# Ten instead of eight head pairs' score maxima in the expert phase of an attention-and-experts kernel, and the output bank zeroed there

## What is computed

```python
zn = layernorm(xn) * ln_w + ln_b
q, k, v = split(zn @ W_qkv + b_qkv)            # 16 heads of 8 columns
attn = softmax(q @ k.T / sqrt(8), over keys)   # 4 batches, 1024 x 1024 per head
s = xn + concat(attn @ v) @ W_proj + b_proj
h = gelu(xn @ W1[e] + b1[e])                   # 8 experts, 512 hidden units
ffn = sum_e weights[:, e] * (h @ W2[e] + b2[e])  # weights: softmax over the top 2 of 8
out = x + s * silu(ffn)
```

## Time and profile before

| | |
|---|---|
| median of three runs | 1101.2 us (1100.84 to 1102.49) |
| the profiled execution's own time | 1103.0 us |
| its span, first to last instruction | 1101.2 us |
| mean granted TensorE clock | 0.988 |
| first exponential (attention begins) | 513.36 us |
| start of block 240 (no more singles) | 1049.36 us |
| PE, DVE, ACT busy over the span | 93%, 80%, 79% |
| PE busy time of matmuls, us | 1029.3 |

### The profile page before, as it was taken

How to read it: one execution, slowest core, us unless ns; L and a number is a source line. 1 busy time by engine, 2 the same in 40 slices (tenths; PEclk the granted TensorE clock), 3 DMA queues, 4 the chain that set the end, 5 groups by cost and what they waited for, 6 DMA issues and landing times.

```text
span 1101.2 us, 17451 instructions
## 1 busy us (share of the span) xinstructions
PE 1029.3 (93%) x5865; PEld 444.1 (40%) x5897; DVE 883.7 (80%) x1589; ACT 866.9 (79%) x1190; POOL 368.0 (33%) x555
## 2 busy tenths in 40 slices
PE   4998999999999999999999999999999999999997
PEld 3675666666666666664222222122222121122222
DVE  5647877787878787765999899989998998899943
ACT  6876667676767677666898998989898989798985
POOL 4786656657666667554001000001000001000010
PEclk9999999999999999999999999999999999999998
DMA  6432221414142232324212221212112221122102
GB/s 183 123 99 68 66 83 31 120 30 121 31 107 50 64 80 51 97 51 120 51 44 53 55 53 39 68 40 54 42 52 51 56 53 42 51 53 54 25 24 82
DMA packets 99410, 72.02 MB, mean 65 GB/s; under 512 B 21693, under 2 KB 83834, under 8 KB 99322
## 3 DMA queue, kind: packets, MB, share of 16 engines
q1 hardware_dynamic: 99322, 70.92, 24.5%
HBM read 53.12 MB, written 15.46 MB: 62 GB/s over the span
## 4 chain that ended last, share of the span: by engine, by line
PE 34%; ACT 8%; DVE 7%; issue 2%; SPq 1%; DMA 0%; POOL 0%; ACTq 0%; DVEq 0%; POOLq 0%
PE psum L1055 17%; PE psum L1034 8%; ACT p_ring L869 8%; PE psum L999 7%; DVE neg_max_half L1318 7%; PE psum L1084 1%; ACT o_sb L860 1%; DMA den<-o_sb 0%; SPq L469 0%; PE psum L1098 0%; PE psum L1010 0%; SPq L473 0%; DVE neg_max_rest L1327 0%; DVE y L1379 0%; POOL h_lo L685 0%
## 5 line engine op out<-in xcount | busy, mean ns | idle before, releaser
L869 ACT ACTIVATE p_ring<-psum 128x1024 f32<-128x1024 f32 x512 | 494.8, 1026 | 59.7 <-PE psum L1034 54.3
L1318 DVE TENSOR_REDUCE neg_max_half<-psum 128x1 f32<-128x512 f32 x768 | 481.6, 681 | 44.5 <-PE psum L999 36.7
L1055 PE MATMUL psum<-p_ring,v_sb 128*9 128x512 f32 x2048 | 269.2, 598 | 0.4 <-ACT o_sb L860 0.3
L823 ACT ACTIVATE h_hi<-psum,cols 128x512 fp32r<-128x512 f32 x192 | 132.4, 690 | 132.2 <-PE psum L949 131.2
L999 PE MATMUL psum<-k_max_stack,q_max_stack 48*128 48x512 bf16 x768 | 202.2, 380 | 16.6 <-DVE neg_max_half L1318 16.3
L1336 DVE TENSOR_REDUCE neg_max_half<-psum 128x1 f32<-128x512 f32 x256 | 169.3, 683 | 51.7 <-PE psum L985 45.0
L685 POOL TENSOR_TENSOR h_lo<-h_split,h_hi 128x512 fp32r<-128x512 f32 x128 | 165.1, 1294 | 135.4 <-ACT h_split L826 135.2
L1034 PE MATMUL psum<-q_stack,k_stack 51*128 51x512 bf16 x1024 | 200.0, 386 | 3.4 <-ACT p_ring L869 2.2
L635 POOL CAST neg_max_parts<-neg_max_rest 128x16 bf16<-128x16 f32 x32 | 6.3, 197 | 493.6 <-DVE neg_max_rest L1327 493.5
L1034 PEld LDWEIGHTS psum<-q_stack,k_stack 51*128 51x128 bf16 x1024 | 49.5, 93 | 299.2 <-ACT p_ring L869 276.2
L947 PE MATMUL psum<-xn_t_hi,w_hi 128*128 128x512 f32 x256 | 144.8, 566 | 0.7 <-DVE neg_max_half L1336 0.5
(11 more groups left out here) (129 smaller groups left out, 957.5 us busy)
## 6 DMA issues: line engine op xcount, KB each, us to landing
expert_w_bc<-expert_w_dram SPq DMA_DIRECT2D x64, 256.0 KB, 5.1
k_rows_dram<-qk_parts SPq DMA_DIRECT2D x24, 256.0 KB, 3.1
q_max_stack<-q_rows_dram SPq DMA_DIRECT2D x64, 96.0 KB, 2.5
k_max_stack<-k_rows_dram SPq DMA_DIRECT2D x64, 96.0 KB, 2.5
q_stack<-q_rows_dram SPq DMA_DIRECT2D x64, 96.0 KB, 2.4
k_stack<-k_rows_dram SPq DMA_DIRECT2D x64, 96.0 KB, 2.5
q_rows_dram<-qk_parts SPq DMA_DIRECT2D x8, 384.0 KB, 2.6
xz<-in_L_attn_z_dram SPq DMA_DIRECT2D x8, 256.0 KB, 3.2
```

Of the source, the lines that this page charges most:

```text
L823: act.activation(hh[:, (g * HS + j) % HR, :], up, ACT.Gelu, bias=col(C_B1 + i))\
L869: act.activation(p_sb[:, n % PR, a, :, :].rearrange("p h t -> p (h t)"), scores_bank[s % 2], ACT.Exp, scale=SCALE).then_inc(S("P"), 1)
L1055: i = pe.matmul(o_bank[at:at + VR, :], v_sb[:, b * KT + kt, 2 * (p % PB) + hh, :], p_sb[:, n % PR, a, hh, :], start=(kt == 0), stop=(kt == ...
L1318: dve.tensor_reduce(mx[:, p % MXR, c, hh * NT + t:hh * NT + t + 1], ring_bank(("max", u)), AX.X, ALU.max, negate=True).then_inc(S("R"), 1)
```

## The change

The first ten pairs' maxima are taken in the expert phase, in the same slots 36 to 251: 320 instead of 256, so 104 of these 216 slots have two (40 before) and the others one. The transpositions' slots are set anew. In the attention phase 704 singles are left instead of 768; they are issued from block 2 to 239 instead of 0 to 239, so that a block has 3 (228 blocks) or 2 (ten blocks) where before it had 3 (192 blocks) or 4 (48). 22 transpositions are left in it instead of 24. The blocks in which a pair is complete move: SP's loads and stores of the maxima move with them. The zeroing of the output bank goes from the head of DVE's attention list to slot 226, behind a wait for the last use of that bank.

```diff
--- before.py
+++ after.py
@@ -182,9 +182,10 @@
 
 
         MAXES = [(p, t, c) for p in range(PAIRS) for t in range(NT) for c in range(2)]
-        EARLY_PAIRS = 8
+        EARLY_PAIRS = 10
         EARLY = EARLY_PAIRS * 4 * NT
         BLOCKS = PAIRS * KT
+        MAX_FROM = 2
         MAX_BLOCKS = BLOCKS - 2 * KT
         RING = []
         ring_at = {}
@@ -194,7 +195,8 @@
 
         def singles_upto(n, half):
 
-            upto = [min(len(SINGLES), -(-((n + a) * len(SINGLES)) // MAX_BLOCKS)) for a in range(2)]
+            upto = [min(len(SINGLES), -(-max(0, n + a - MAX_FROM) * len(SINGLES) // (MAX_BLOCKS - MAX_FROM)))
+                    for a in range(2)]
             return (upto[0], min(upto[0] + 2, upto[1]), upto[1])[half]
 
         def done_block(p):
@@ -223,9 +225,10 @@
                 on_ring(item)
         ENDS_FROM = BLOCKS - 2 * KT + 3
 
-        EARLY_AT = [HT + 4 + (27 * m) // 32 for m in range(EARLY)]
+        EARLY_AT = [HT + 4 + (27 * m) // 40 for m in range(EARLY)]
         EARLY_DONE = [EARLY_AT[(p + 1) * 4 * NT - 1] for p in range(EARLY_PAIRS)]
-        EARLY_TURN = [2 * HT + 2, 2 * HT + 28, 3 * HT + 26, 4 * HT + 26, 5 * HT + 26, 6 * HT + 26, 7 * HT + 5, 8 * HT + 1]
+        EARLY_TURN = [g * HT + at for g, at in ((1, 28), (2, 26), (3, 26), (3, 30), (4, 26), (5, 26), (5, 30), (6, 26),
+                                                (7, 9), (7, 30))]
         EARLY_MIN = [d + 2 for d in EARLY_DONE]
 
         def ring_bank(item):
@@ -547,19 +550,20 @@
                     sp.wait_ge(S("qp_st"), 2 * QP_ST)
                     for p in range(2):
                         sp_max_rows(sp, p)
-                if g in (2, 3):
-                    sp_max_rows(sp, g)
+                for p in {2: [2], 4: [5], 6: [8]}.get(g, []):
+                    sp_max_rows(sp, p)
                 if g + 1 < NG:
                     sp_load_x(sp, g + 1)
                 spread_w(g)
-                if g > 2:
-                    sp_max_rows(sp, g + 1)
-                for p in ([], [], [0], [1], [2], [3], [4], [5, 6])[g]:
+                for p in {2: [3], 3: [4], 4: [6], 5: [7], 6: [9]}.get(g, []):
+                    sp_max_rows(sp, p)
+                for p in {2: [0], 3: [1], 4: [2, 3], 5: [4], 6: [5, 6], 7: [7, 8]}.get(g, []):
                     sp_store_max(sp, p)
+            sp_max_rows(sp, EARLY_PAIRS)
             for p in range(2):
                 sp_score_rows(sp, p)
                 sp_load_max(sp, p)
-            sp_store_max(sp, 7)
+            sp_store_max(sp, EARLY_PAIRS - 1)
             sp.wait_ge(S("qp_st"), NG * QP_ST)
             sp_max_rows(sp, EARLY_PAIRS + 1)
             sp.wait_ge(S("m2"), NG * HT)
@@ -1340,7 +1344,12 @@
             def lo(ns):
                 return [lambda n=n: weights_lo(dve, n) for n in ns]
 
-            beside = {}
+            def o_zero():
+
+                dve.wait_ge(S("vd"), NG)
+                dve.memset(o_bank[:, :], 0.0).then_inc(S("o_zero"), 1)
+
+            beside = {(NG - 1) * HT + 2: [o_zero]}
             for m in range(EARLY):
                 beside.setdefault(EARLY_AT[m], []).append(early_max(m))
             for p in range(EARLY_PAIRS):
@@ -1402,7 +1411,6 @@
                 ends.setdefault(4 * g + 2, []).append(lambda g=g: finish(g))
 
             dve.wait_ge(S("vd"), NG)
-            dve.memset(o_bank[:, :], 0.0).then_inc(S("o_zero"), 1)
             for n in range(BLOCKS):
                 halves, turns = block_items(n)
                 p, kt = divmod(n, KT)
```

## The result

The changed kernel takes 1106.12 us (median of five runs, 1104.33 to 1107.32); its ratio to the kernel before is 1.0037 [1.0026, 1.0048]. The forecast was 1096 and a small gain; it is a small loss. The profiled execution took 1104.33 us, span 1102.5, clock 0.993. TensorE, VectorE and ScalarE are busy for 93, 79 and 79% of it.

What follows compares the result with a forecast made beforehand. TensorE was taken to pace the expert phase, ScalarE the attention blocks with three singles. 14.1 + 11 + 1 - 2.4 - 34.7 + 6.2 = -4.8 us from 1103.0 gave 1098.2, by median 1096, range 1083 to 1108.

Steps and rivals of the forecast that it cites:

- I take +11: Expert phase: VectorE's crowding by 64 added reductions (full slots, waits for two banks) costs +11 us.
- 64 x 0.22 = +14.1: Expert phase: TensorE's own work for 64 further maxima at 0.22 us each, +14.1 us.
- I take +1: Turns (transpositions of pairs' maxima): a 3.2 us stop before slot 254, partly regained elsewhere; +1 us, between -2 and +3.
- E as a whole, +26: E, the stretch from slot 32's `up` to the first exponential, grows by 26 us.
- -2.4: Start of attention: without memset and singles in blocks 0 and 1, the first blocks take 6.3 us; -2.4 us.
- -34.7: Attention, blocks 3 to 239: with three singles or two per block, 492.6 instead of 527.3 us; -34.7 us.
- +6.2: Attention, SP at kt = 2: late denominators in five pairs make VectorE, then TensorE wait; +6.2 us, 0 to 12.
- TensorE's wait near 23: Expert phase: TensorE's total wait for the early maxima's reductions, 12.2 us before, comes near 23.
- the second (1105): Rival, VectorE binds the expert phase: TensorE's waits for reductions grow by 19.5 us; 1105 us, chance 0.25.
- The third: Rival, attention: denominators come late in more pairs, 12 us lost instead of 6.2; 1102 us, chance 0.10.
- the fourth: Rival: TensorE binds both phases, attention gives back only 7 us; 1124 us, chance 0.04.
- the gaps take the reductions: Rival, expert phase: VectorE's idle gaps absorb added reductions, +3 instead of +11, late denominators cost 2; 1084 us, chance 0.20.

Runs made afterwards that it cites:

- e3: Changed kernel (ten early pairs) with each early reduction over 256 of its 512 keys, the other half left out: 1094.32 us, ratio 0.9935.
- e4: Kernel before (eight early pairs) with each early reduction over 256 of its 512 keys: 1094.12 us, ratio 0.9926.
- e6: Changed kernel with the same 320 early maxima, second ones mainly in slots 3 and 0 modulo four, three turns later: 1076.69 us, ratio 0.977.
- e10: Changed kernel with VectorE's low half of the split one slot later in its list, no maximum moved: 1088.11 us, ratio 0.9883.
- e8: Kernel before (eight early pairs) with memset in slot 226, singles from block 2, SP's sums and denominators first: 1099.63 us, ratio 0.998.
- e5: Changed kernel again, unaltered, on a second chip: 1103.35 us, ratio 1.0019 to the kernel before.
- e1: Changed kernel with pair 9's turn back in the tail (slot 257 instead of 254): 1100.04 us, ratio 0.9984.
- e7: Changed kernel with second maxima in better slots, pair 9's turn in the tail, and SP's sums and denominators first: 1067.54 us, ratio 0.9692.
- e2: Changed kernel with SP's issues of sums and denominators ahead of its loads and stores of maxima: 1099.01 us, ratio 0.9965.
- e12: Kernel before with memset in slot 226, singles from block 2, SP's sums first, and 40 second maxima in slots 3 modulo four: 1090.76 us, ratio 0.9904.

## Why the prediction was wrong, point by point

- **"I take +11" for VectorE, the step that failed: its size held by luck, its reason did not.** It said that a further maximum pays its whole reduction where VectorE is full, and that the 12.2 us of waits grow with the double slots. Measured, 28.4 us of E less 14.1 and less 3.0 for the turns leave 11.3. But with VectorE 61 us less busy the 64 maxima still cost 26.4 instead of 28.4 us (e3, e4), and with as many doubles the waits are 2.4 us instead of 17.6 and E 25.9 us shorter (e6). Without a maximum moved, the low half one slot later in VectorE's list gives 14.2 us (e10). The price is one of the order in VectorE's list, and a term for that was missing. "64 x 0.22 = +14.1" for TensorE's own work was not tried by itself: well placed, 64 maxima cost 10.6 us in all.
- **What a further maximum costs, from the trace.** e8 has the early maxima in the places of the kernel before. In its groups 1 to 6 the time from the start of the matmul ahead to a maximum's start is 77.1 us over 224 maxima (0.344 each), in e5 101.5 over 280. The 56 further ones cost 24.4 us, 0.44 each, and the groups themselves are 24.6 us longer (400.0 against 375.4).
- **"I take +1" for the turns: mis-sized.** A wait of 3.2 us in slot 254 was forecast, and 3.09 came; 2.5 to 3.8 are a loss (e1). Not foreseen was pair 0's turn, four slots behind its last maximum, where TensorE waited 1.41 us; pair 2's 0.52 came in the first profile and not in e5. Less 1.63 and 0.36 that went at pairs 1 and 6, the waits grew by 3.0, the upper bound given.
- **E as a whole, +26: measured +28.4 and +30.0.** The turns are 2 us of the 2.4 above the forecast. Of the 28.4, 22.5 lie in groups 1 to 6 and 5.9 behind slot 224.
- **"-2.4" for the start of attention: -1.7** (6.99 instead of 8.72 us). e8, with eight pairs, the early memset and the empty blocks, has 7.22. No run tries the memset or the empty blocks alone. The forecast of 6.3 us took no account of the clock: before and after, 3.4 us of this stretch are at 1.2 GHz; e7, with none, takes 5.77.
- **"-34.7" and "+6.2": right.** Blocks 3 to 239 took 499.5 us, forecast 492.6 + 6.2 = 498.8. The late denominators came in pairs 4, 11, 15 and 27 (1.42, 1.06, 0.95, 1.35 us of VectorE's wait) and not in pair 8; in four other pairs before block 240 VectorE waited about 0.5. e2 puts them at 5.4 to 7.3 us in all.
- **"TensorE's wait near 23", "first exponential about 539".** 18.7 and 544.05; 2.2 of the latter lie before slot 32.
- **From the profile to the median.** In the profiled executions the change is +1.3 us against -4.8: +2.2 (start) + 2.4 (E) + 1.4 (A) + 0.1. The medians differ by 4.9, because the profiled execution of before lay 1.8 us above its median and that of after 1.8 below. The forecast took 1.8 off and could not know the second. So of the miss of 10.1 us, 6.1 lie in the four stretches of the table (2.2 of them in the start, which e5 shows to be no part of the change), 3.6 between single executions and medians, and 0.4 in 1096.4 taken as 1096.
- **The rivals.** In size the second (1105) came true, by luck and not by its own cause: TensorE's waits for reductions grew by 6.5 us and not by over 15.8. The third is out by e2 (7.3 us at most, not 12), the fourth by A, which gave 29.5 us and not 7. The first, "the gaps take the reductions", is wrong of the change and right of e6: the gaps do take them once the order lets them.

A sum of +32.3 (14.1, 11, 1, 6.2) and -37.1 (2.4, 34.7) with 5 us of doubt in each does not settle a sign. Beside the mechanism the chances were at fault: 0.52 for faster rests on a net of -4.8 that is no larger than the doubt about it.

That a maximum costs TensorE twice as much in the expert phase, as the Trainium skill, TensorEngine Tiling, section "Theoretical Speedup", has it of contractions of 64 rows, holds in the trace (0.22 us for two singles, 0.22 for one more maximum). Yet e7 has 64 more of them there than e12 and is 2.1% faster (ratios 0.9692 and 0.9904): in attention they cost more than TensorE's work, since blocks with four singles are slower than ScalarE's 1.95 us, and in E the gaps take part of the price.

## What to carry to other kernels

When work is added to an engine that executes its list in order, look at what stands ahead of each added instruction and what that waits for, not at the engine's busy share: VectorE was 76% busy, and the places of the second maxima were worth 26 us, from worst to best 41. A steady wait for a reduction with a small number of banks calls for the slot-by-slot timeline of both engines. Moving the waiting instruction behind the ready one gave 14 us here, what it delayed included. And where a change takes 30 us from one phase and puts 30 into another, look for what the dearer half pays without need (here placement made a loss of 0.2 to 0.4% into a gain of 2.3%), and don't stake much on the sign of the difference.

## What was not expected of the hardware

- Two profiled executions of one kernel differ by as much as the turn in slot 254 costs: start to slot 32 took 80.4 us in one execution of the changed kernel and 77.9 in the other, for a reason that stays open. The mean granted clock of the two was 0.993 and 0.988 of full speed. Both have a few short stretches at the lower level, 1.2 GHz, in different places: in E none in the first, two of 3.4 us in the second.
- In five of eight executions a stop of TensorE of 3.1 us went along with a stretch of 3.4 us at 1.2 GHz, so that the stop cost up to 4.0 us.
- A wait table counts part of a loss: 15.2 us of waits went in e6 where 25.9 us of time did.
